# Order of SP's issues behind the rounds of a post-norm decoder layer: last transposes ahead of the early expert weights, and three small codes later on DVE

## What is computed

```
x = layernorm(x + attention(x))              # 16 heads of 64, with biases
x = layernorm(x + cross(ctx, ctx, x, mask))  # one head of 64
x = layernorm(x + experts(x))                # 32 experts, top 8, capacity 512
```

## Time and profile before

| | us |
|---|---|
| median of 3 runs | 1873.47 (1871.95 to 1873.96) |
| the profiled execution | 1876.34 |
| span in its trace | 1874.6 |
| PE busy | 1784.7 (95%) |
| DVE busy | 1300.8 (69%) |
| ACT busy | 1144.4 (61%) |
| POOL busy | 653.9 (35%) |
| mean granted TensorE clock | 0.985 of full speed |

### The profile page before, as it was taken

One profiled execution on the slowest core, in us unless ns is written; L12 is line 12 of the kernel. 1 busy time (PEld: TensorE's weight loads), 2 busy tenths in 40 slices (PEclk: granted clock), 3 DMA queues, 4 the chain that ended last, 5 costly groups with the idle time before them and its releaser, 6 DMA issues.

```text
span 1874.6 us, 38873 instructions
## 1 busy us (share of the span) xinstructions
PE 1784.7 (95%) x13111; PEld 1023.4 (55%) x13111; DVE 1300.8 (69%) x2712; ACT 1144.4 (61%) x2884; POOL 653.9 (35%) x556
## 2 busy tenths in 40 slices
PE   7899999999999999999999889999999999999992
PEld 4566666666666666666665444444444444444441
DVE  6667989898989898989898864444444444444464
ACT  7877887798879877987797433333333333333344
POOL 1111111121112111211121145555655555555545
PEclk9999999999999999999999999999999999999996
DMA  7646765766476647664767399999999999999996
GB/s 215 160 79 124 153 126 105 160 141 136 101 161 141 134 102 162 140 136 100 163 129 155 106 236 269 246 242 233 240 243 234 235 249 232 240 246 228 249 268 265
DMA packets 597206, 341.38 MB, mean 182 GB/s; under 512 B 492832, under 2 KB 523552, under 8 KB 597152
## 3 DMA queue, kind: packets, MB, share of 16 engines
q1 hardware_dynamic: 567760, 267.28, 60.3%
q0 software_dynamic: 29392, 73.42, 17.5%
HBM read 160.77 MB, written 61.34 MB: 118 GB/s over the span
## 4 chain that ended last, share of the span: by engine, by line
PE 64%; DVE 12%; issue 7%; SPq 5%; ACT 5%; DMA 5%; POOL 2%; DVEq 0%; ACTq 0%; POOLq 0%
PE bank L686 37%; PE bank L1151 12%; PE bank L774 8%; DVE stage L1606 2%; PE bank L763 2%; PE bank L739 2%; DMA x1T<-x1h 2%; SPq L499 2%; ACT arena_p L1249 1%; ACT stage L1270 1%; ACT arena_q L1230 1%; SPq L489 1%; DVE s_neg L1642 1%; SPq L501 1%; DMA arena_p<-stage 1%
## 5 line engine op out<-in xcount | busy, mean ns | idle before, releaser
L2350 POOL TENSOR_TENSOR arena_q<-arena_q 128x512 f16<-128x512 f32 x128 | 167.3, 1307 | 818.4 <-ACT arena_q L1230 714.6
L1606 DVE SCALAR_TENSOR_TENSOR arena_wo<-stage,arena_wo 128x3072 f16<-128x3072 f32 (+3 forms) x78 | 182.4, 2342 | 287.2 <-ACT arena_wo L1338 265.2
L686 PE MATMUL bank<-xt,arena_wo 128*128 128x256 f16 x2688 | 314.4, 274 | 1.9 <-ACT arena_q L1230 1.9
L686 PEld LDWEIGHTS bank<-xt,arena_wo 128*128 128x128 f16 x2688 | 258.8, 98 | 55.4 <-issue 14.7
L2428 POOL DMA_INDIRECT acc_rows<-arena_wo,cur_to x120 | 192.3, 1603 | 235.6 <-ACT arena_wo L1582 218.1
L1151 PE MATMUL bank<-arena_wo 128*128 128x512 f16 x1152 | 256.1, 381 | 3.5 <-DVE z L1990 2.0
L686 PE MATMUL bank<-arena_v,arena_wo 128*128 128x512 f16 x1152 | 251.6, 379 | 0.2 <-issue 0.2
L686 PE MATMUL bank<-arena_q,arena_wo 128*128 128x512 f16 x1152 | 251.2, 379 | 0.0
L1249 ACT ACTIVATE arena_p<-bank,s_neg 128x256 f32<-128x256 f32 x508 | 233.7, 481 | 25.4 <-DVE s_neg L1642 23.7
L1230 ACT ACTIVATE arena_q<-bank,bqkv 128x256 f32<-128x256 f32 (+1 forms) x512 | 201.8, 490 | 73.1 <-PE bank L686 72.7
L1606 DVE SCALAR_TENSOR_TENSOR stage<-arena_p,s_rden,stage 128x256 f16<-128x256 f32 x508 | 211.6, 478 | 28.0 <-ACT stage L1270 28.0
(11 more groups left out here) (281 smaller groups left out, 2352.2 us busy)
## 6 DMA issues: line engine op xcount, KB each, us to landing
stage<-wguT SPq DMA_DIRECT2D x31, 1536.0 KB
stage<-wdnT SPq DMA_DIRECT2D x32, 768.0 KB, 5.6
xt<-xT SPq DMA_DIRECT2D x16, 512.0 KB, 4.8
xr<-x_rows SPq DMA_DIRECT2D x16, 512.0 KB, 4.2
stage<-ctxT SPq DMA_DIRECT2D x16, 512.0 KB, 3.8
acc_rows<-x SPq DMA_DIRECT2D x15, 512.0 KB, 2.9
x_rows<-stage SPq DMA_DIRECT2D x30, 256.0 KB, 3.7
arena_p<-stage SPq DMA_TRANSPOSE x256, 3.1
```

Source lines behind the costliest of these rows:

```text
L686: mm = pe.matmul(out_ap, lhs(a, i), rhs(c, i), start=(n == 0 and i == 0), stop=(n == 2 and i == chunks - 1))
L1606: return vec.scalar_tensor_tensor(out=dst, in0=src, scalar=scale, in1=hi, op0=ALU.mult, op1=ALU.subtract)
L2350: gp.tensor_tensor(qk[:, j % 2, 1, :], qk32[:, j % 2, :], qk[:, j % 2, 0, :], ALU.subtract).then_inc(qk_lo, 1)
```

## The change

SP issues the two early loads of expert 0's weights behind `turn_x1(u)` instead of between the turns of pairs `EC - 3` and `EC - 2`. DVE makes the late codes behind `heads_lo(b, EC - 5)` instead of at the head of its drain.

```
@@ SP, drain @@
                 turn(b, EC - 3)
+                turn(b, EC - 2)
+                turn(b, EC - 1)
+                turn_x1(u)
                 first_weights(DC - 1, DC, ld_early)
                 sp.dma_start(stage[:, 0, WGU:NW].rearrange("p (c n) -> p c n", c=FC),
                              wdnT[0].rearrange("(c p) n -> p c n", p=P)).then_inc(ld_early, 16)
-                turn(b, EC - 2)
-                turn(b, EC - 1)
-                turn_x1(u)
                 turn_x2(f)
@@ DVE, drain @@
                 b, u, f = LAST, LAST - 1, LAST - 2
-                late_codes()
                 maxima(b, EC - 2)
                 probs_lo(b, EC - 3)
                 row_scales(b, EC - 2)
                 heads_lo(b, EC - 5)
+                late_codes()
                 dve.wait_ge(s_mm, count(b, EC, EC))
```

## The result

The change made the kernel slower: 1878.33 us by median (1874.98 to 1885.57, 11 runs) against 1873.19 us (1871.2 to 1874.48, 11 runs) of the kernel before, a ratio of 1.0035 with a 95% interval of 1.0026 to 1.0045. That is 5.1 us by the medians and 6.6 by the ratio, where 2.5 us were forecast; the median lies just above the top of the range. In a later series (e13) the same pair gave 1878.11 against 1873.46 us, 1.0023 (1.0012 to 1.0034). The runs of the changed kernel lie 10.6 us apart where those of before lie 3.3 apart; in the later series it was 10.3 us against 8.8 (11 and 35 runs), so the wider spread is less sure than the loss.

What follows compares the result with a forecast made beforehand. Only the drain mattered, its chain running through SP's transposes, then DVE. Terms: 0 (PE's 2.5 us covered) + 1.9 (late weights) + 0.6 (clock) = +2.5 us, so 1876.0 us, range 1872.0 to 1878.2.

Steps and rivals of the forecast that it cites:

- SP and the transposes: SP's drain queue: transposes of the last two pairs go sooner, last weigh at 1024.4 us, gaining PE 2.5 us.
- That data is then the limit: Last pair's transposes on SP: limited by halves ready at 1018.9 and 1020.6 us, not SP; last issued 1.6 us earlier.
- What is late next: Drain, ACT and DVE: weights land at 1030.8 to 1031.6 us, residuals wait for them, 1.5 to 2.3 us lost.
- The codes: DVE's drain: moving three additions is worth 0.24 us to PE's list, bounds 0.24 either way, zero at the end.
- The clock: PE in the drain: idle 4.3 us, then low clock over about 1.3 us of needed work, priced at +0.6 us.
- Slower by over 0.2%: Rival at ACT's weight wait: landing past about 1032 us, low clock costing 1.3 us; +4.0 us or more; chance 0.17.
- (1): Sign on SP: transposes of the last two pairs held about 1.3 us, not 3.40, last issued near 1020.5.
- (2): Sign on PE: weigh of the last pair near 1024.4 us with little or no wait.
- (3): Sign on SP: the early load L590 issued near 1025 us and the weights landing near 1031.
- (4): Sign on ACT: a new wait of about 5 us for the weights' DMA, with DVE's piece behind it.
- (6): Sign on PE: a hole of about 4 us near 1032 to 1036 us, a clock of 0.50 behind it.
- (5): Sign on DVE: residuals near 1033 us, behind DVE's own piece and not behind PE.

Runs made afterwards that it cites:

- e13: The whole change run once more, against the kernel before on the same chip: 1878.11 us, 1.0023.
- e1: Only SP's new order of the change, late codes at their old place, against the kernel before: 1882.00 us, 1.0050.
- e3: The whole change plus 14 matmuls keeping PE busy ahead of cross_scores(u), against the kernel before: 1877.66 us, 1.0033.
- e7: The two loads between the turns of the last pair and turn_x1(u), against the kernel before: 1875.09 us, 1.0009.
- e9: The two loads two transposes later than in the change, behind turn_x2(f), against the kernel before: 1880.90 us, 1.0038.
- e10: As e5, plus seven matmuls keeping PE busy ahead of weigh of the fourth pair, against the kernel before: 1872.66 us, 0.9994.
- e12: The change plus PE-busy matmuls, seven ahead of weigh of the fourth pair and 14 ahead of cross_scores(u), against the kernel before: 1875.43 us, 1.0010.
- e2: Only DVE's moved codes, SP's order as before, against the kernel before: 1873.88 us, 1.0004.
- e4: The whole change, but ACT's first piece of early weights waits for its own load alone, against the kernel before: 1877.26 us, 1.0022.
- e5: SP's new order, with ACT's and DVE's pieces of the early weights moved behind the residuals, against the kernel before: 1872.37 us, 0.9992.
- after: The changed kernel as first profiled, against the kernel before: profiled execution 1883.38 us, median 1878.33 us.
- e6: The whole change, but POOL issues the two early loads at the head of its drain, against the kernel before: 1875.45 us, 1.0006.

## Why the prediction was wrong

- **SP and the transposes: right, but for one wait.** The hold fell from 3.40 to 1.23 us. Where no low clock came in between (e1, e3, e7, e9, e10, e12), the last `weigh` ran at 17.7 to 17.9 us of the drain, 2.3 to 2.5 us sooner; 2.5 was forecast. In the two profiles of the change itself it ran at 20.9 and 19.5 us against 20.2 before, so little or nothing of that was left. "That data is then the limit" left out that the turn of the last pair also waits for `weigh` of `EC - 3`, which was the limit in the profiled run.
- **What is late next: right, with its size.** ACT waits for the weights, DVE's piece stands ahead of the residuals. Forecast 1.5 to 2.3 us, measured 1.6 (e12), 2.2 (e1), 2.4 (e3) us; e12's runs put the price on the whole time at 2.0 us. e1's drain began within 0.2 us of before's, so its times can be held against the forecast ones: the last transpose at 1020.87 us (1020.5), the last `weigh` at 1024.37 (1024.4), the gate and up load at 1024.96 (1024.6 to 1025.4), the landing at 1031.3 (1030.8 to 1031.6), the residuals at 1033.12 (1032.6 to 1033.4). The prediction's estimate from the Trainium skill's page DMA: Bandwidth & Descriptors, a landing at 1030.1 us, was not met.
- **The codes: right** in the old order of SP (e2, no effect by the runs). With the loads late it is open, since e1 was slower than the change.
- **The clock: the step that failed.** "I price it at +0.6 us", with bounds of 0 and 1.3, from 1.3 us of PE's work at low clock. The clock did fall, as forecast, but the term was far too small. The low clock behind the hole lasted 13.7 us in both profiles of the change, not the 3.4 us of each low stretch in the trace of before, and covered transposes, queries, bias rows and scores of the last sequence; it cost 3.0 us in these profiles. A term was missing as well: a low clock at the first wait of the drain, behind 1.82 us of idle, which the trace of before did not show though its wait was 2.05 us. It held `weigh` of `EC - 3`, with it ACT's norm of x1 and the transposes of x1, and so pushed the loads: 2.1 us more at the residuals in the profiled run (28.7 against e1's 26.6). It occurs in the profiles of e4, e5, after and e13 and not in e1, e2, e3, e6, e7 and e9. By the runs (e13 against e12, likely and not proved; e3's median does not show it) the two low clocks together are worth 2.7 us, where +0.6 stood in the sum; the wait alone is worth 2.0 (e12), where +1.9 stood. That accounts for most of the 2.6 us by which the median passed the forecast. The rule on idle gaps that the prediction quoted from the Trainium skill's page TensorE: Matmul & The Clock Gate was right in sign behind the hole (3.49 us idle, then 0.50); the price, which I took from one short stretch, was the mistake.
- **The rivals.** "Slower by over 0.2%" came true. It had 0.17, and its price, +4.0 us or more, was met. Its condition on the clock held, and in the profiled run its decisive point too, a landing past 1032 us (1032.7), but not for its reason: L499 held SP 1.28 us, and the loads went 2 us later because of the early low clock. In e1 the landing was 1031.3 us and the time was over that price all the same.
- **Numbered signs.** (1) held for the time SP was held, though the last transpose of the pair was issued at 1022.60, not near 1020.5. (2) held without a wait, but at 1026.7 us. (3) was late by 2 us. (4) and (6) came as written, with a hole of 3.49 us that ended at 1037.9. (5) came behind DVE's own piece, but at 1034.5 us.

## What to carry to other kernels

When a load is moved behind other work on a queue, look for the instruction that needs it and for what stands behind that instruction in its engine's list, before counting what the queue gains; here the 2.5 us that PE gained (e1) were worth nothing, since DVE stood for the weights. The consumer whose data came later had to move too (e5); left in its place, it cost more than the move gave. And when a change opens a new idle time of TensorE, do not price the clock by one low stretch of another place: here it was 3.4 us long in one profile with the hole and 13.7 to 17.1 in three, so the price is a range, and wide.

## What the runs showed beyond that

- The low clock need not end with the hole: from 1036.4 us it lasted 13.7 us while PE was counted busy for 2.8 of 3 us in 1038 to 1041 us. Work at half speed looks busy, so the busy share does not show a low clock; the granted clock does.
- The second DMA transpose issued behind 1 MB or so of plain loads was held on SP for 2.3 to 4.5 us: 2.32 and 2.42 us behind the context's and rows' loads, 3.31 (in the change), 3.40 and 4.26 us behind the weights from SP, 4.47 us behind the context's and rows' loads with the weights from POOL. The other transposes of these drains were held 1.23 to 2.2 us, but for one of 2.89 us in e6.
- Executions of one program on one core differ by 3 to 16 us here (3.3 us in 11 runs of before, 13.1 in 33 of them, 16.1 in 12 of e7). The length of the drain changes with where the low clock falls, and in e1 the experts took 2.7 us longer than before.
